# The quantised feed-forward of layer 2: one pipeline over four batch elements, with the depthwise convolution taken into three matmuls

## Chip, cores and metric

The kernel runs on one core of one Trainium2 chip. The metric is the device time of one execution in microseconds (us). It is a whole small model of some fourteen sublayers, and the change touches one of them, called L2f in the code.

## What is computed

Per batch element x is 512 tokens by 128 features, and there are four elements. L2f is a feed-forward with "bit-linear" layers (the reference, cut):

```python
def act_quant(x):                     # per token
    scale = 127.0 / clip(max(abs(x), axis=-1), 1e-05)
    return clip(round(x * scale), -128, 127) / scale
def weight_quant(w):                  # one scale for the matrix
    scale = 1.0 / clip(mean(abs(w)), 1e-05)
    return clip(round(w * scale), -1, 1) / scale
def bit_linear(x, w):
    return einsum('bsd,hd->bsh', act_quant(x), weight_quant(w))

h = bit_linear(x, w1)                 # 128 -> 512
h = depthwise_conv1d(h, conv_w, conv_b)   # 3 taps along the tokens, padding 1
h = silu(h)
return bit_linear(h, w2)              # 512 -> 128
```

The result is added to x and layer-normalised. All arithmetic of this part is float32.

## The kernel before, in words

Activations are kept feature-major: a tile has 128 features on the partitions and 512 tokens along the row. The program is a list of sublayers. Ahead of each, `turn` (L120) waits for that sublayer's weight pack, which lies in one of two arenas in SBUF, and issues the DMA of the next sublayer's pack into the other (L131). A sublayer is made of stages. A stage (`core.stage`, L116) is a block in which every engine runs its own list of instructions, ordered by semaphores; no engine goes on to the next stage before all have ended this one. Each engine is a queue in program order. `Chain` (L41) makes VectorE wait for each of its own instructions before the next, where the next reads what it wrote.

`each(bit_ffn)` (L3102) runs `bit_ffn` (L2972) for the four elements in turn, and then one residual-and-norm over all of them. For one element `bit_ffn` has six stages:

1. `quantize_weights` (L2884): ScalarE takes the absolute values of w1 and w2 with a running sum (L2900), TensorE adds the sums over the partitions (L2905), VectorE makes mean and inverse and quantises each 128x512 matrix in three passes: scale and round (L2915), subtract and clip (L2916), clip and scale back (L2917). It is done anew for each element, with the same result.
2. `quantize_tokens` (L2920) of x: TensorE transposes four 128x128 tiles so that tokens lie on the partitions (L2937); VectorE, tile after tile, takes the maximum (L2953), four operations on one column (L2955 to L2958) and three passes over the tile (L2959, L2961, L2962); when all four tiles are done TensorE transposes them back (L2943) and ScalarE copies them to SBUF (L2969).
3. `dense` (L224): four products with the chunks of w1, read out in turn by ScalarE and VectorE. A float32 product of 128x128 by 128x512 shows as two MATMUL records.
4. The convolution: VectorE, three passes for each of the four 128-feature chunks of the 512 hidden features (L2997, and L3000 twice); ScalarE applies SiLU to each chunk (L3012).
5. `quantize_tokens` of the hidden features: as stage 2 with sixteen transposes each way and tiles of 128x512.
6. `dense` with w2: four products added up in one bank, copied to `core.sums` (L261).

Of the kernel before, what the change touches and what calls it, by code (L numbers as in the profile page):

```python
# [8 lines left out]
P = 128  # L9
B, S, D = 4, 512, 128  # L10
TILE = 128
QT = S // TILE
# [2868 lines left out]
ROUND = 1.5 * 2.0 ** 23  # L2881


def quantize_weights(core, raw, out):  # L2884

    nc = core.nc
    with core.stage() as st, nc.sbuf_tensor(f"wq_abs{nc.next_id()}", [P, 2, 512], F32) as mag, \
            nc.sbuf_tensor(f"wq_sum{nc.next_id()}", [P, 2], F32) as sums, \
            nc.sbuf_tensor(f"wq_mean{nc.next_id()}", [P, 2], F32) as mean, \
            nc.sbuf_tensor(f"wq_inv{nc.next_id()}", [P, 2], F32) as inv:  # L2890
        sums_ready, total_ready, step = st.sem("sums_ready"), st.sem("total_ready"), st.sem("step")

        @st.block.sync
        def _(sp):
            sp.sem_clear(st.stale)

        @st.block.scalar
        def _(act):
            for i in range(2):
                nc.scalar.activation(mag[:, i, :], raw[i], ACT.Abs, accum_out=sums[:, i:i + 1]).then_inc(sums_ready, 1)  # L2900

        @st.block.tensor
        def _(pe):
            pe.wait_ge(sums_ready, 2)
            nc.tensor.matmul(core.ps[0][:, 0:2], core.c("ones"), sums[:, :], start=True, stop=True)\  # L2905
              .then_inc(total_ready, 1)

        @st.block.vector
        def _(dve):
            link = Chain(dve, step)  # L2910
            dve.wait_ge(total_ready, 1)
            link(nc.vector.tensor_scalar(mean[:, :], core.ps[0][:, 0:2], 1.0 / (P * 512), 1e-5, ALU.mult, ALU.max))
            link(nc.vector.reciprocal(inv[:, :], mean[:, :]))
            for i in range(2):
                link(nc.vector.tensor_scalar(out[i], raw[i], inv[:, i:i + 1], ROUND, ALU.mult, ALU.add))  # L2915
                link(nc.vector.tensor_scalar(out[i], out[i], ROUND, 1.0, ALU.subtract, ALU.min))  # L2916
                link(nc.vector.tensor_scalar(out[i], out[i], -1.0, mean[:, i:i + 1], ALU.max, ALU.mult))  # L2917


def quantize_tokens(core, src, dst, chunks):  # L2920

    nc = core.nc
    width = chunks * P
    with core.stage() as st, nc.sbuf_tensor(f"tq{nc.next_id()}", [P, QT, width], F32) as q, \
            nc.sbuf_tensor(f"tq_max{nc.next_id()}", [P, QT], F32) as top, \
            nc.sbuf_tensor(f"tq_scale{nc.next_id()}", [P, QT], F32) as scale:
        turned, step, quantized, back, evac = (st.sem(n) for n in ("turned", "step", "quantized", "back", "evac"))

        @st.block.sync
        def _(sp):  # L2930
            sp.sem_clear(st.stale)

        @st.block.tensor
        def _(pe):
            for t in range(QT):
                for c in range(chunks):
                    mm = nc.tensor.transpose(core.ps[t][:, c * P:(c + 1) * P], src[:, c, t * P:(t + 1) * P],  # L2937
                                             core.ident)
                mm.then_inc(turned, 1)
            pe.wait_ge(quantized, QT)  # L2940
            for c in range(chunks):
                for t in range(QT):
                    mm = nc.tensor.transpose(core.ps[4 + c][:, t * P:(t + 1) * P], q[:, t, c * P:(c + 1) * P],  # L2943
                                             core.ident)
                mm.then_inc(back, 1)

        @st.block.vector
        def _(dve):
            link = Chain(dve, step)
            for t in range(QT):  # L2950
                dve.wait_ge(turned, t + 1)
                one = slice(t, t + 1)
                link(nc.vector.tensor_reduce(top[:, one], core.ps[t][:, 0:width], AX_X, ALU.max,  # L2953
                                             apply_absolute_value=True))
                link(nc.vector.tensor_scalar(top[:, one], top[:, one], 1e-5, None, ALU.max))  # L2955
                link(nc.vector.reciprocal(scale[:, one], top[:, one]))
                link(nc.vector.tensor_scalar(scale[:, one], scale[:, one], 127.0, None, ALU.mult))
                link(nc.vector.tensor_scalar(top[:, one], top[:, one], 1.0 / 127.0, None, ALU.mult))  # L2958
                link(nc.vector.tensor_scalar(q[:, t, :], core.ps[t][:, 0:width], scale[:, one], ROUND,  # L2959
                                             ALU.mult, ALU.add))  # L2960
                link(nc.vector.tensor_scalar(q[:, t, :], q[:, t, :], ROUND, 127.0, ALU.subtract, ALU.min))  # L2961
                nc.vector.tensor_scalar(q[:, t, :], q[:, t, :], -128.0, top[:, one], ALU.max, ALU.mult)\  # L2962
                  .then_inc(quantized, 1)

        @st.block.scalar
        def _(act):
            for c in range(chunks):
                act.wait_ge(back, c + 1)
                nc.scalar.copy(dst[:, c, :], core.ps[4 + c][:, :]).then_inc(evac, 1)  # L2969


def bit_ffn(core, b, arena):  # L2972
    nc = core.nc
    w = core.weights("L2f", arena)
    M = 4
    with ExitStack() as mem:
        def tmp(name, shape):
            return mem.enter_context(nc.sbuf_tensor(f"l2f_{name}_{nc.next_id()}", shape, F32))
        W, xq = tmp("W", [P, 2, 512]), tmp("xq", [P, 1, S])
        h, z, hq = tmp("h", [P, M, S + 2]), tmp("z", [P, M, S]), tmp("hq", [P, M, S])  # L2980
        quantize_weights(core, [w("w1"), w("w2")], [W[:, i, :] for i in range(2)])
        quantize_tokens(core, core.X.unsqueeze(1), xq, 1)
        dense(core, M, lambda k, m: W[:, 0, m * P:(m + 1) * P], lambda k: xq[:, 0, :], lambda m: h[:, m, 1:S + 1])
        with core.stage() as st:
            step, conv_ready, silu_ready = (st.sem(n) for n in ("step", "conv_ready", "silu_ready"))

            @st.block.sync
            def _(sp):
                sp.sem_clear(st.stale)

            @st.block.vector
            def _(dve):
                link = Chain(dve, step)
                link(nc.vector.memset(h[:, :, 0:1], 0.0))
                link(nc.vector.memset(h[:, :, S + 1:S + 2], 0.0))
                for m in range(M):
                    link(nc.vector.tensor_scalar(z[:, m, :], h[:, m, 0:S], w("conv_w", 3 * m, 3 * m + 1),  # L2997
                                                 w("conv_b", m, m + 1), ALU.mult, ALU.add))
                    for j in (1, 2):
                        ins = nc.vector.scalar_tensor_tensor(  # L3000
                            out=z[:, m, :], in0=h[:, m, j:j + S], scalar=w("conv_w", 3 * m + j, 3 * m + j + 1),
                            in1=z[:, m, :], op0=ALU.mult, op1=ALU.add)
                        if j == 1:
                            link(ins)
                        else:
                            ins.then_inc(conv_ready, 1)

            @st.block.scalar
            def _(act):
                for m in range(M):  # L3010
                    act.wait_ge(conv_ready, m + 1)
                    nc.scalar.activation(z[:, m, :], z[:, m, :], ACT.Silu).then_inc(silu_ready, 1)  # L3012
# [185 lines left out]
def cols_of(v):  # L3198

    return v.reshape(-1, P).T  # L3200
# [51 lines left out]
def packs(x):  # L3252
# [158 lines left out]
```

## Time and profile before

| | |
|---|---|
| Runs shown | 5674.03, 5654.67, 5646.64 us; median 5654.67 |
| The profiled execution | 5665.67 us |
| Its span in the trace | 5663.4 us |
| TensorE busy, share of the span | 4616.4 us, 82% |
| VectorE | 3167.7 us, 56% |
| ScalarE | 2854.6 us, 50% |
| GpSimd | 1976.5 us, 35% |
| Mean granted TensorE clock | 0.883 of full speed |

The span is that of one execution as the hardware profiler saw it; 2.3 us of the time lie outside it. Busy times are of the whole program, so they say little about one sublayer; the views of the stretch from 4494 to 4726 us, in which L2f runs, do. In the traces PE is TensorE's matmuls, PEld its weight loads, DVE VectorE, ACT ScalarE, POOL GpSimd and SP the queue that issues the DMAs. A granted clock of 1.00 is 2.4 GHz and 0.50 is 1.2 GHz.

### The profile page before, as it was taken

To read this page: it belongs to the slowest core of one execution; us is meant where nothing else is said; L and a number is where in the kernel's file an instruction comes from. 1 tells how busy PE (TensorE), PEld (TensorE's weight loads), DVE (VectorE), ACT (ScalarE), POOL (GpSimd) and SP (SyncE) were. 2 spreads that over 40 slices of the span, in tenths; PEclk is the share of its full clock that TensorE was granted. 3 is DMA by queue.
4 is the path that set the end of the run, shared out by engine and by line. 5 is a ranking of instruction groups with operands and counts; after the bars stand their busy time and mean duration, and the time that the engine had idled before them with its cause. 6 is when DMAs were issued, how large, how long until landed. Compare 5 with 4: busy or idle time off the path is not lost. (4 is left out here: it accounts for less than half of the span.)

```text
span 5663.4 us, 100659 instructions
## 1 busy us (share of the span) xinstructions
PE 4616.4 (82%) x36210; PEld 2809.5 (50%) x36210; DVE 3167.7 (56%) x6182; ACT 2854.6 (50%) x8728; POOL 1976.5 (35%) x2119
## 2 busy tenths in 40 slices
PE   3998779997988979889798899655589736888888
PEld 1665346565655646646466465344466522224433
DVE  6452245455756747567476575399945554654333
ACT  2452234455756747667476574477724312543411
POOL 0230000136939839579396692033213200000000
PEclk6999979899999999999999998767689856997888
DMA  0000000001111111111112111000000000001000
GB/s 32 22 1 4 15 11 7 17 2 27 45 40 41 45 42 44 44 37 45 37 45 55 31 45 34 19 1 1 1 5 1 4 0 7 9 3 34 3 0 8
DMA packets 34488, 122.26 MB, mean 22 GB/s; under 512 B 8484, under 2 KB 9512, under 8 KB 32424
## 3 DMA queue, kind: packets, MB, share of 16 engines
q1 hardware_dynamic: 33960, 115.44, 7.6%
q8 instruction: 304, 4.98, 0.4%
q14 instruction: 224, 1.84, 0.1%
HBM read 36.45 MB, written 1.05 MB: 7 GB/s over the span
## 5 line engine op out<-in xcount | busy, mean ns | idle before, releaser
L640 POOL MEMSET norm_eps<- 128x1 f32 x16 | 1.6, 98 | 1920.0 <-POOLq L116 1861.0
L2095 POOL TENSOR_TENSOR local_other<-local_raw,local_sin 128x256 f32<-128x256 f32 x768 | 557.3, 726 | 60.2
L1956 PE MATMUL ps<-arena,local_xs 128*128 128x512 f32 x768 | 440.3, 658 | 109.5 <-DVE local_raw L2136 60.4
L2092 POOL TENSOR_TENSOR local_rot<-local_raw,local_cos 128x512 f32<-128x512 f32 x384 | 488.2, 1271 | 68.3 <-DVE local_raw L2136 68.2
L2098 POOL TENSOR_TENSOR local_rot<-local_rot,local_other 128x512 f32<-128x512 f32 x384 | 486.6, 1267 | 30.1
L2069 ACT ACTIVATE ps<-ps,local_negmax 128x96 f32<-128x96 f32 x1536 | 474.2, 309 | 41.0 <-DVE local_negmax L2130 41.0
L2136 DVE SCALAR_TENSOR_TENSOR local_raw<-local_inverse,ps 128x512 f32<-128x512 f32 x384 | 264.1, 688 | 274.1 <-ACT local_inverse L2063 274.1
L2126 DVE TENSOR_REDUCE local_norm<-local_squares 128x8 f32<-128x512 f32 x384 | 263.2, 685 | 133.6 <-ACT local_squares L2038 133.6
L2069 ACT ACTIVATION_READ_ACCUMULATOR ps<-ps,local_negmax 128x1 f32 x1536 | 309.8, 202 | 0.0
L2038 ACT ACTIVATE local_squares<-ps 128x512 f32<-128x512 f32 x384 | 229.8, 598 | 158.5 <-PE ps L1956 158.3
L2001 PE MATMUL ps<-const,local_probs 128*96 128x128 f32 x1536 | 237.0, 276 | 75.7 <-DVE local_probs L2154 75.7
L1985 PE MATMUL ps<-const,local_rot 128*128 128x128 f32 x1536 | 245.9, 282 | 45.1 <-POOL local_rot L2098 45.0
L1985 PEld LDWEIGHTS ps<-const,local_rot 128*128 128x128 f32 x1536 | 175.1, 141 | 188.0 <-POOL local_rot L2098 92.8
L2001 PEld LDWEIGHTS ps<-const,local_probs 128*96 128x96 f32 x1536 | 171.9, 126 | 192.6 <-DVE local_probs L2154 100.6
L2014 PE MATMUL ps<-local_pts,local_V_span 96*64 96x64 f32 x6144 | 266.5, 230 | 0.5
L2014 PEld LDWEIGHTS ps<-local_pts,local_V_span 96*64 96x64 f32 x6144 | 213.2, 139 | 71.0 <-issue 69.9
L2077 ACT COPY local_pts<-ps 96x512 f32<-96x512 f32 x384 | 221.4, 577 | 17.6 <-PE ps L2001 17.6
L1432 DVE TENSOR_REDUCE l3a_limits<-ps 128x1 f32<-128x512 f32 x256 | 165.0, 686 | 111.5 <-PE ps L1280 111.5
L2047 ACT ACTIVATE local_Q<-ps 128x512 f32<-128x512 f32 x192 | 114.6, 597 | 217.4 <-PE ps L1985 217.4
L2154 DVE TENSOR_TENSOR local_probs<-ps,local_total 128x384 f32<-128x384 f32 x384 | 214.1, 557 | 13.3
L2130 DVE TENSOR_REDUCE local_negmax<-ps 128x4 f32<-128x384 f32 x384 | 210.4, 548 | 7.4 <-PE ps L1974 7.4
L1956 PEld LDWEIGHTS ps<-arena,local_xs 128*128 128x128 f32 x768 | 119.4, 195 | 180.8 <-DVE local_raw L2136 105.1
(510 smaller groups left out, 11083.9 us busy)
## 6 DMA issues: line engine op xcount, KB each, us to landing
local_V_span<-local_V SPq DMA_DIRECT2D x96, 384.0 KB, 4.0
local_V_span<-local_V SPq DMA_DIRECT2D x96, 256.0 KB, 3.6
arena<-in_L1f_a SPq DMA_DIRECT2D x7, 2176.0 KB, 8.3
local_V_span<-local_V SPq DMA_DIRECT2D x72, 128.0 KB, 2.3
arena<-in_L3f SPq DMA_DIRECT2D x1, 3460.0 KB, 11.3
arena<-in_L1f_f SPq DMA_DIRECT2D x6, 537.5 KB, 3.9
arena<-in_L0f SPq DMA_DIRECT2D x1, 2824.5 KB, 9.9
arena<-in_L0x SPq DMA_DIRECT2D x1, 2049.5 KB, 9.1
```

The source lines that it names most:

```text
L1956: nc.tensor.matmul(bank("qk", n)[:, :], tokens_of(tile), w("Wqkv", QKV[i] * 512, (QKV[i] + 1) * 512), start=True, stop=True)\
L1985: mm = nc.tensor.transpose(TURN[:, c * P:(c + 1) * P], m.rot[:, n % 4, c * P:(c + 1) * P], core.ident)
L2001: mm = nc.tensor.transpose(PT[0:SPAN, u * P:(u + 1) * P], m.probs[:, g % 2, u, :], core.ident)
L2014: mm = nc.tensor.matmul(OUT[DH * h:DH * h + DH, c * SPAN_Q:(c + 1) * SPAN_Q], m.V_span[:, tile % 2, half_span, (2 * c + h) * DH:(2 * c + h ...
L2038: nc.scalar.activation(m.squares[:, n % 2, :], bank("qk", n)[:, :], ACT.Square).then_inc(squared, 1)
L2069: nc.scalar.activation(scores, scores, ACT.Exp, bias=m.negmax[:, s % 2, u:u + 1], accum_out=m.total[:, s % 2, u:u + 1])\
L2077: nc.scalar.copy(m.pts[:, g % 3, :, :].rearrange("p u q -> p (u q)"), PT[0:SPAN, :])\
L2092: link(nc.gpsimd.tensor_tensor(rot, raw, m.cos[:, t, a * DH:(a + 1) * DH].unsqueeze(1) .broadcast_to([P, 8, DH]), ALU.mult))
L2095: link(nc.gpsimd.tensor_tensor(other[:, :, lo:lo + HALF], raw[:, :, HALF - lo:DH - lo], m.sin[:, t, a * DH + lo:a * DH + lo + HALF].unsque ...
L2098: nc.gpsimd.tensor_tensor(rot, rot, other, ALU.add).then_inc(rotated, 1)
L2126: nc.vector.tensor_reduce(m.norm[:, n % 4, :], heads(m.squares[:, n % 2, :]), AX_X, ALU.add)\
L2136: nc.vector.scalar_tensor_tensor(out=heads(m.raw[:, n % 4, :]), in0=m.inverse[:, n % 4, :].unsqueeze(2).broadcast_to([P, 8, DH]), scalar=1 ...
```

## The change

- The list of sublayers names `bit_ffn_all` in the place of `each(bit_ffn)`. It has one stage for all four elements, followed by the same residual-and-norm.
- Weights are quantised once. The first matrix, quantised, is multiplied by the convolution's weights into three matrices `taps` (VectorE, three `tensor_tensor` of 128x512). For this the host puts `conv_rows`, 1536 columns, into the pack of L2f; the old `conv_w` stays in it.
- The first product and the convolution are one: for each chunk TensorE adds three products in one bank, one per tap, of `taps[j]` with the quantised x read from column j of a buffer of 514 columns whose edge columns are zero (GpSimd writes them). ScalarE applies SiLU with the bias as it reads the bank.
- The four single-column operations of a quantisation are done once for four tiles, on four columns.
- Every engine's order is written out for steps s = 0 to 4: TensorE does the products of element s, the transposes of its hidden features, then the transposes back and the second products of element s-1, and the transposes back of x for element s+1. VectorE quantises the hidden features of element s and then x of element s+2. Two banks of PSUM serve the first products and the transposes back in turn, four hold the transposed hidden features, one x and one the last product.

The core of the diff:

```diff
-def bit_ffn(core, b, arena):
-        quantize_weights(core, [w("w1"), w("w2")], [W[:, i, :] for i in range(2)])
-        quantize_tokens(core, core.X.unsqueeze(1), xq, 1)
-        dense(core, M, lambda k, m: W[:, 0, m * P:(m + 1) * P], lambda k: xq[:, 0, :], lambda m: h[:, m, 1:S + 1])
...
-        quantize_tokens(core, z, hq, M)
-        dense(core, 1, lambda k, m: W[:, 1, k * P:(k + 1) * P], lambda k: hq[:, k, :], lambda m: core.Y[:, :],
-              kcount=M)
+def bit_ffn_all(core, _, arena):
...
+            def convolve(b, m):
+                wait_bank(("hidden", b, m))
+                pe.wait_ge(x_read, b + 1)
+                for j in range(TAPS):
+                    mm = nc.tensor.matmul(place["hidden", b, m][:, :], taps[:, j, m * P:(m + 1) * P],
+                                          x_quant[:, b % 2, j:j + S], start=(j == 0), stop=(j == TAPS - 1))
+                mm.then_inc(hidden_ready, 1)
+
+            def turn_hidden(b):
+                pe.wait_ge(hidden_read, M * (b + 1))
+                for t in range(QT):
+                    if b >= 1:
+                        pe.wait_ge(tile_read, QT * (b - 1) + t + 1)
+                    for c in range(M):
+                        mm = nc.tensor.transpose(TURNED[t][:, c * P:(c + 1) * P], z[:, c, t * P:(t + 1) * P], core.ident)
+                    mm.then_inc(turned, 1)
+
+            def back_hidden(b, c):
+                wait_bank(("back", b, c))
+                pe.wait_ge(rows_ready, QT * (b + 1))
+                for t in range(QT):
+                    mm = nc.tensor.transpose(place["back", b, c][:, t * P:(t + 1) * P],
+                                             rows[:, b % 2, t, c * P:(c + 1) * P], core.ident)
+                mm.then_inc(back_ready, 1)
...
+            turn_x(0)
+            pe.wait_ge(sums_ready, 2)
+            nc.tensor.matmul(OUT[:, 0:2], core.c("ones"), sums[:, :], start=True, stop=True).then_inc(total_ready, 1)
+            back_x(0)
+            turn_x(1)
+            pe.wait_ge(edges, 2)
+            pe.wait_ge(taps_ready, TAPS)
+            for s in range(B + 1):
+                if s < B:
+                    for m in range(M):
+                        convolve(s, m)
+                        if m == 1 and s >= 1 and s + 1 < B:
+                            turn_x(s + 1)
+                    turn_hidden(s)
+                if s >= 1:
+                    if s == 1:
+                        pe.wait_ge(second_ready, 1)
+                    back_hidden(s - 1, 0)
+                    back_hidden(s - 1, 1)
+                    for c in range(M):
+                        if c + 2 < M:
+                            back_hidden(s - 1, c + 2)
+                        project(s - 1, c)
+                if s + 1 < B:
+                    back_x(s + 1)
...
+            def scales():
+                link(nc.vector.tensor_scalar(top[:, :], top[:, :], 1e-5, None, ALU.max))
+                link(nc.vector.reciprocal(scale[:, :], top[:, :]))
+                nc.vector.tensor_scalar(unit[:, :], top[:, :], 1.0 / 127.0, None, ALU.mult).then_inc(step, 1)
+                link.steps += 1
+                link(nc.vector.tensor_scalar(scale[:, :], scale[:, :], 127.0, None, ALU.mult))
...
+            def quantize_hidden(b):
+                for t in range(QT):
+                    dve.wait_ge(turned, QT * b + t + 1)
+                    link(nc.vector.tensor_reduce(top[:, t:t + 1], TURNED[t][:, :], AX_X, ALU.max,
+                                                 apply_absolute_value=True))
+                scales()
+                for t in range(QT):
+                    here, one = rows[:, b % 2, t, :], slice(t, t + 1)
+                    nc.vector.tensor_scalar(here, TURNED[t][:, :], scale[:, one], ROUND, ALU.mult, ALU.add)\
+                      .then_inc(tile_read, 1)
+                    dve.wait_ge(tile_read, QT * b + t + 1)
+                    link(nc.vector.tensor_scalar(here, here, ROUND, 127.0, ALU.subtract, ALU.min))
+                    nc.vector.tensor_scalar(here, here, -128.0, unit[:, one], ALU.max, ALU.mult).then_inc(rows_ready, 1)
+
+            quantize_x(0)
+            dve.wait_ge(total_ready, 1)
...
+            quantize_weights(0)
+            for j in range(TAPS):
+                nc.vector.tensor_tensor(taps[:, j, :], whole[:, 0, :], w("conv_rows", j * 512, (j + 1) * 512), ALU.mult)\
+                  .then_inc(taps_ready, 1)
+            quantize_x(1)
+            quantize_weights(1)
+            for b in range(B):
+                quantize_hidden(b)
+                if b + 2 < B:
+                    quantize_x(b + 2)
+    residual_norm_all(core, core.sums)
...
-             ("L2f", each(bit_ffn)), ("L3a", projected_attention), ("L3x", cross_narrow), ("L3f", each(experts))]
+             ("L2f", bit_ffn_all), ("L3a", projected_attention), ("L3x", cross_narrow), ("L3f", each(experts))]
...
+    p.add("conv_rows", np.tile(x["L2_ffn_conv_w"][:, 0, :].T.reshape(1, -1), (P, 1)))
```

ScalarE's list in the new stage: absolute sums of both matrices, the copy of x(0), then per step four SiLUs of element s, four copies of the transposed-back hidden features of element s-1, the copy of its result to `core.sums`, and the copy of x for element s+1.

## Rows read from the trace of the kernel before

**Rows 1.** Busy time by engine (count), granted clock, DMA share, GB/s, L2f's stretch.

```profile
4494.00:4726.00 232.00, 86.43 (x232) 51.36 (x232) 124.62 (x354) 35.96 (x66) 0.10 (x1) 0.59 0.01 2
```

**Rows 2.** Longest waits, 4494 to 4728 us: total, times, longest.

```profile
PE ps L2943 <- DVE tq L2962: 69.7, 8, 10.2
...
ACT l2f_hq L2969 <- PE ps L2943: 64.3, 16, 15.3
```

**Rows 3.** Timeline, element 0, and the last copy of element 3: start, duration.

```profile
4495.02 0.63 ACT L2900 ACTIVATE wq_abs<-arena 128x512 f32<-128x512 f32 x1 [2.74 <-PEq L122]
...
4509.29 1.12 PE L2943 MATMUL ps<-const,tq 128*128 128x128 f32 x4 [7.27 <-DVE tq L2962]
4510.45 0.58 ACT L2969 COPY l2f_xq<-ps 128x512 f32<-128x512 f32 x1 [14.10 <-PE ps L2943]
...
4511.34 5.46 PE L251 MATMUL ps<-l2f_xq,l2f_W 128*128 128x512 f32 x8 [0.93 <-PEq L116]
...
4527.31 3.65 PE L2937 MATMUL ps<-const,l2f_z 128*128 128x128 f32 x16 [10.50 <-PEq L116]
...
4529.92 0.75 DVE L2959 TENSOR_SCALAR tq<-ps,tq_scale 128x512 f32<-128x512 f32 x1
4530.71 0.43 DVE L2961 TENSOR_SCALAR tq<-tq 128x512 f32<-128x512 f32 x1
4531.17 0.49 DVE L2962 TENSOR_SCALAR tq<-tq,tq_max 128x512 f32<-128x512 f32 x1
4531.57 0.69 DVE L2953 TENSOR_REDUCE tq_max<-ps 128x1 f32<-128x512 f32 x1
...
4533.05 0.75 DVE L2959 TENSOR_SCALAR tq<-ps,tq_scale 128x512 f32<-128x512 f32 x1
...
4724.75 0.60 ACT L261 ACTIVATE sums<-ps 128x512 f32<-128x512 f32 x1 [6.11 <-PE ps L251]
```

**Rows 4.** Groups of VectorE by shape, 4494 to 4728 us: busy us, mean ns.

```profile
L3000 DVE SCALAR_TENSOR_TENSOR l2f_z<-l2f_h,arena,l2f_z 128x512 f32<-128x512 f32 x32 | 24.1, 752 | 1.1
...
L2959 DVE TENSOR_SCALAR tq<-ps,tq_scale 128x128 f32<-128x128 f32 x16 | 5.6, 351 | 0.6
...
L2962 DVE TENSOR_SCALAR tq<-tq,tq_max 128x128 f32<-128x128 f32 x16 | 4.6, 286 | 0.6
L2915 DVE TENSOR_SCALAR l2f_W<-arena,wq_inv 128x512 f32<-128x512 f32 x8 | 3.9, 487 | 0.3
L2961 DVE TENSOR_SCALAR tq<-tq 128x128 f32<-128x128 f32 x16 | 3.6, 227 | 0.6
```

**Rows 5.** Timeline, state-space sublayer L2a: products with shifted windows, SiLU with bias.

```profile
3578.81 7.03 PE L2463 MATMUL ps<-ssm_xn,ssm_taps 128*128 128x512 f32 x16
3585.68 1.88 PE L2466 MATMUL ps<-ssm_xn,arena 128*128 128x512 f32 x4
...
3577.29 0.69 ACT L2486 ACTIVATE ssm_XC<-ps,arena 128x512 f32<-128x512 f32 x1 [2.75 <-PE ps L2463]
```

**Rows 6.** Timeline, local attention: four transposes at full clock, and what follows.

```profile
2511.10 0.66 PE L1985 MATMUL ps<-const,local_rot 128*128 128x128 f32 x4
2511.59 0.59 PE L1992 MATMUL ps<-arena,local_xs 128*128 128x512 f32 x1
```

**Rows 7.** One line's instructions, L394 (elementwise product in SBUF): ns min/median/max.

```profile
L394 DVE TENSOR_TENSOR rwkv_num<-rwkv_num,rwkv_kv x4: 691/692/692, 28.7 to 113.7; 128x512 f32<-128x512 f32 x4
```

**Rows 8.** As Rows 1, microseconds after and long after products at L251.

```profile
4515.00:4516.00 1.00, 1.00 (x4) 0.49 (x3) 0.69 (x1) 0.02 (x1) 0.00 (x0) 1.00 0.00 0
4521.00:4522.00 1.00, 0.00 (x0) 0.00 (x0) 0.96 (x2) 0.00 (x0) 0.00 (x0) 0.89 0.00 0
```

**Rows 9.** Page, DMA issues (KB, us to landing), and the issue of L2f's pack.

```profile
arena<-in_L1f_a SPq DMA_DIRECT2D x7, 2176.0 KB, 8.3
...
arena<-in_L2f SPq DMA_DIRECT2D x1, 520.0 KB, 3.6
...
4172.23 0.33 SPq L131 DMA_DIRECT2D arena<-in_L2f  x1
```

More of the change, by code:

```diff
@@ L2881, with tmp @@
 ROUND = 1.5 * 2.0 ** 23
-def quantize_weights(core, raw, out):
+ROUND = 1.5 * 2.0 ** 23
+def bit_ffn_all(core, _, arena):
     nc = core.nc
[L2887 to L2891, printed above, removed]
+    w = core.weights("L2f", arena)
+    M, TAPS = 4, 3
+    TURNED, RING, ROWS, OUT = core.ps[0:4], core.ps[4:6], core.ps[6], core.ps[7]
+    uses = []
+    for s in range(B + 1):
+        uses += [("hidden", s, m) for m in range(M) if s < B] + [("back", s - 1, c) for c in range(M) if s >= 1]
+    place = {use: RING[n % 2] for n, use in enumerate(uses)}
+    held = {use: uses[n - 2] for n, use in enumerate(uses) if n >= 2}
+    with core.stage() as st, ExitStack() as mem:
+        def tmp(name, shape):
+            return mem.enter_context(nc.sbuf_tensor(f"l2f_{name}_{nc.next_id()}", shape, F32))
+        mag, sums, mean, inverse = tmp("mag", [P, 2, 512]), tmp("sum", [P, 2]), tmp("mean", [P, 2]), tmp("inverse", [P, 2])
+        whole, taps = tmp("whole", [P, 2, 512]), tmp("taps", [P, TAPS, 512])
+        x_rows, x_quant = tmp("x_rows", [P, 2, QT, P]), tmp("x_quant", [P, 2, S + 2])
+        z, rows, quant = tmp("z", [P, M, S]), tmp("rows", [P, 2, QT, 512]), tmp("quant", [P, M, S])
+        top, scale, unit = tmp("top", [P, QT]), tmp("scale", [P, QT]), tmp("unit", [P, QT])
+        step, sums_ready, total_ready, taps_ready, second_ready, edges, x_turned, x_ready, x_back, x_read = (
+            st.sem(n) for n in ("step", "sums_ready", "total_ready", "taps_ready", "second_ready", "edges", "x_turned",
+                                "x_ready", "x_back", "x_read"))
+        hidden_ready, hidden_read, turned, rows_ready, back_ready, back_read, projected, stored, tile_read = (
+            st.sem(n) for n in ("hidden_ready", "hidden_read", "turned", "rows_ready", "back_ready", "back_read",
+                                "projected", "stored", "tile_read"))
         @st.block.sync
@@ L2897, in _, with read_x @@
         @st.block.scalar
         def _(act):
[L2899 to L2906, printed above, removed]
+            def read_x(b):
+                act.wait_ge(x_back, b + 1)
+                nc.scalar.copy(x_quant[:, b % 2, 1:S + 1], ROWS[:, :]).then_inc(x_read, 1)
@@ new lines, in _ @@
+            for i, name in enumerate(("w1", "w2")):
+                nc.scalar.activation(mag[:, i, :], w(name), ACT.Abs, accum_out=sums[:, i:i + 1]).then_inc(sums_ready, 1)
+            read_x(0)
+            for s in range(B + 1):
+                if s < B:
+                    for m in range(M):
+                        act.wait_ge(hidden_ready, M * s + m + 1)
+                        if m == 0 and s >= 1:
+                            act.wait_ge(turned, QT * s)
+                        nc.scalar.activation(z[:, m, :], place["hidden", s, m][:, :], ACT.Silu,
+                                             bias=w("conv_b", m, m + 1)).then_inc(hidden_read, 1)
+                if s >= 1:
+                    for c in range(M):
+                        act.wait_ge(back_ready, M * (s - 1) + c + 1)
+                        if c == 0 and s >= 2:
+                            act.wait_ge(projected, s - 1)
+                        nc.scalar.copy(quant[:, c, :], place["back", s - 1, c][:, :]).then_inc(back_read, 1)
+                    act.wait_ge(projected, s)
+                    nc.scalar.copy(core.sums[:, s - 1, :], OUT[:, :]).then_inc(stored, 1)
+                if s + 1 < B:
+                    read_x(s + 1)
@@ L2910, in _ @@
             link = Chain(dve, step)
-            dve.wait_ge(total_ready, 1)
[L2912 to L2917, printed above, removed]
@@ L2920, in quantize_tokens @@
[L2920 to L2969, printed above, removed]
@@ new lines, in quantize_weights @@
+            def quantize_weights(i):
+                out = whole[:, i, :]
+                link(nc.vector.tensor_scalar(out, w(("w1", "w2")[i]), inverse[:, i:i + 1], ROUND, ALU.mult, ALU.add))
+                link(nc.vector.tensor_scalar(out, out, ROUND, 1.0, ALU.subtract, ALU.min))
+                ins = nc.vector.tensor_scalar(out, out, -1.0, mean[:, i:i + 1], ALU.max, ALU.mult)
+                if i == 0:
+                    link(ins)
+                else:
+                    ins.then_inc(second_ready, 1)
@@ new lines, in _ @@
+            quantize_x(0)
+            dve.wait_ge(total_ready, 1)
+            link(nc.vector.tensor_scalar(mean[:, :], OUT[:, 0:2], 1.0 / (P * 512), 1e-5, ALU.mult, ALU.max))
+            link(nc.vector.reciprocal(inverse[:, :], mean[:, :]))
+            quantize_weights(0)
[3 more added lines that the diff above has]
+            quantize_x(1)
```

79 lines of the change are left out of this document (45 added, 34 removed).

## The prediction

> **What bounds the kernel now.** I read the busy times of the sublayer's stretch first, then its waits, then the timeline of one element. In the 232 us of L2f no engine comes near its limit: VectorE is busy 124.6 us (54%), TensorE 86.4 (37%), ScalarE 36.0, with TensorE's clock at a mean of 0.59 [rows 1]. So the work is a chain handed from engine to engine. The waits say the same: TensorE stood 69.7 us in eight waits for VectorE's quantising, and ScalarE 64.3 us for transposes whose own release was that quantising [rows 2]. The reader is to see waits that all end on the engine before in the chain, and none on a DMA. The chain runs from ScalarE's first instruction at 4495.02 to the end of the last copy at 4724.75 + 0.60 = 4725.35, thus 230.3 us, four times some 57.6 [rows 3]. What counts is how long the new chain is between these two points; the program before and after is the same.
>
> **Prices.** A float32 product of 128x512 at full clock: sixteen records (eight products) from 3578.81 to 3585.68, 0.86 us each [rows 5]; those are products with windows shifted by single columns, as here. At half clock twice that, 1.71. A transpose at full clock: four from 2511.10 to 2511.59, 0.12 each, 0.49 for four [rows 6]; at half clock sixteen take 3.65 with their end, about 0.21 each [rows 3]. From the end of four slow transposes (0.85) to ScalarE's read: 4510.45 - 4509.29 - 0.85 = 0.31 us, taken for each read of a bank [rows 3]. A copy 0.58, SiLU with bias out of PSUM 0.69 [rows 3, 5]; I add 0.05 to each for the signal back. VectorE on 128x512: from start to start 0.79 for the first pass (it reads PSUM), 0.46 the second, 0.40 the third where the next does not need it; maximum plus four column operations 4533.05 - 4531.57 = 1.48, of which 0.72 the maximum and 0.19 each of the four [rows 3]. On 128x128: 0.35, 0.23 and 0.29 [rows 4], 0.99 for the three with 0.04 for each link.
>
> **The change part by part**, times from the first instruction (0), at full clock unless said.
>
> Start. x(0) is turned (1.2, clock low); maximum and column operations 1.5 (the four columns of 128 are one reduction of 512 elements); twelve passes 4 x 0.99 = 4.0; mean and inverse 0.4. TensorE's sum over the absolute values lies under this. w1 in three passes of 0.53 + 0.46 + 0.53 = 1.5, by 487 ns for the outer ones [rows 4] and 0.46 for the middle. **The three products into `taps`** are new: nearest row 692 ns, 2.1 for three [rows 7]. If they cost as the slowest two-input pass here, 0.75, it is 0.2 more; below 0.69 no row of that size goes, and even at nothing it is 2.1 less. The sum is 10.7. The transposes back and the copy of x(0), 2.1, end under w1. ScalarE's table load can cost 1.3 at most, and ScalarE has idle time there.
>
> Products of element 0: 12 x 0.86 = 10.3. Before, eight records starting at 4511.34 went from low clock to high, and the microsecond from 4515 had it at 1.00 [rows 3, 8]; so about 3.5 us go at half speed, 1.75 more, to 22.8. The last SiLU 0.31 + 0.69 + 0.05 = 1.05, and `turn_hidden(0)` starts at 23.8. Sixteen transposes 1.96, x(1) back and copied 0.49 + 0.31 + 0.63 = 1.4, products of element 1 with x(2) turned among them 10.3 + 0.5, SiLU 1.05: `turn_hidden(1)` starts at 39.0. x(1) and w2, 6.9 us on VectorE, are done by 17.6 and so cost nothing; their cover is the products of element 0.
>
> One step from there: transposes 1.96; two chunks back 0.98; the third needs the bank of the first, 0.31 + 0.63 after it, so 0.46 of waiting; the rest 2 x 0.49 + 4 x 0.86 = 4.4; then the products of the next element wait for x, and ScalarE's copy of it stands behind the copy of the result: 0.31 + 0.65 + 0.63 = 1.6; products and x turned 10.8; SiLU 1.05. Together **21.3 us on TensorE**. VectorE in one step: four maxima 2.9, columns 0.76, four tiles of 1.65 = 6.6, together 10.3; x 5.5; sum 15.8. It fits, and each wait is met: quantised rows are needed some 21 us after the turn begins and are ready after 11, and x(s+2) is turned in the middle of the products and ready 5.5 later, before the next hidden tile comes. The new wait of `turn_hidden` for `tile_read` has behind it on TensorE the whole of the next step, but VectorE has read those tiles 10 us before. So turns start at 39.0, 60.3 and, without an x to turn, 81.1.
>
> End. After the last turn VectorE needs 0.8 + 10.3, until 92.1, and TensorE, done with element 2 at 88.9, stands 3.2. Then 5.9 for chunks and products and 0.9 for the copy: **98.9 us**, in the place of 230.3. Saved: 131.4.
>
> Off the path: the convolution's 12 passes per element on VectorE (L2997, and L3000 of 752 ns [rows 4]) and 24 stages less 1 with their boundaries are in the 230.3 and need no term. SP: the pack of L2f grows by 1536 columns, 768 KB, to 1288 KB. 520 KB landed 3.6 us and 2176 KB 8.3 us after issue, and L2f's is issued at 4172.23, over 300 us before its use [rows 9]: nothing. The next pack is issued as before at the head of the sublayer, and 99 us cover it. GpSimd's two small memsets are under the first 10 us.
>
> The profiled execution took 5665.67 us, of which its span is 5663.4; less 131 it is 5534. The median of the runs shown is 11.0 below it, 5654.67; less 131 it is **5524 us**.
>
> **The rivals.**
> (A) The clock doesn't stay. Between the products of one element and the next there are 1.05 of waiting, 1.96 and 0.98 of transposes and 0.46 of waiting, 4.4 us without a product, and before the last chunks 3.2 us of idleness. For it: in the old kernel sixteen transposes from 4527.31 ran their whole 3.65 us at half clock, and the clock fell within 4521 to 4522 after some 5 us without work [rows 3, 8]. Against it: here TensorE works in 17.6 of 21.3 us, and its waits are 1.6 at most until the end. Priced with everything but the products of w1 at half clock: turns 4 x 1.5, chunks back and second products (10.3 for 5.9) 4 x 4.5, and each of three later elements climbs anew, 3 x 1.75: 29 us, so 5553. The rule of the Trainium skill, "TensorE: Matmul & The Clock Gate", section "A second HAM failure mode: psum-queue depth-cycling", speaks for this rival: short idle times between groups of matmuls that rotate through PSUM banks can make the clock go back and forth. By that rule the time would be nearer 5553 than 5524; no row here shows such a rotation with full 128-row products losing the clock. If the clock stayed low all the time: products of w1 4 x 20.6, turns 13.6, chunks and second products 41, and 22 of waits: 159 us, 5583.
> (B) The elements don't overlap, because a wait in one of the three hand-written orders stands ahead of what the other engine needs (VectorE has the hidden features of b ahead of x of b+2). Then each element costs its own chain, 8 + 13 + 11 + 7 = 39, and 156 in all: 5580. I find no such wait.
> (C) Slower than before: TensorE reading x_quant from an odd column is slow. Place: the 48 products of `convolve`, 96 records of 0.43 us. To end 0.5% slower the stage would have to take 258 us, 159 more than reckoned, 1.7 per record: it decides from 2.1 us for a record, five times the price. At ten times it would be 371 us more than my sum, about 5895. Against it stands the L2a stage, which reads windows at one-column steps at 0.86 a product [rows 5].
> (D) It saves what it says only in part: if the quantised weights alone counted, some 6 us for each of three elements, 18 of 5655, that is no change.
>
> **How the numbers follow.** Forecast 0.76; (A) 0.14; clock low throughout or (B) 0.05; (D) or something of its size 0.03; (C) 0.02. Range: below, the sum may be wrong by 2.1 for taps and by the 0.31 and 0.05 counted in some 25 reads, 8 us together, and the median of a few runs lies some 8 us about its place (the runs shown spread over 27): 5508. Above it takes in (A) and some of that spread: 5565. Changes of 0.5%, 28 us, are about what a measurement of this kernel can tell: faster than 5626 in all but (C) and (D).
>
> **What would show it.** The stretch of L2f is 99 us (95 to 130) from the first absolute sum to the last copy to `sums`, in one stage; SiLUs of successive elements 21 us apart; TensorE over 80% busy at a clock near 1.00 from some 4 us after the first product; the largest waits of VectorE for `turned`, of TensorE for the first element's taps (10 us) and for the last rows (3 us). Wrong if the records of the products are far from 0.43 us apart, if the clock in the steps is under 0.9 (A), if the SiLU groups come over 30 us apart (B), or if other sublayers change by more than a few us.

## The result, and the profile after

The changed kernel took 5528.99 us, median of four runs (5521.40 to 5533.31), against 5659.44 for the kernel before in four (5646.64 to 5674.03). The ratio is 0.9767, 95% interval 0.974 to 0.9795. Forecast was 5524 us and, against the median then known, a ratio of 0.977.

The profiled execution has 5529.55 us and a span of 5527.8, 135.6 less than before. Where those 135.6 us lie is read from the stretch of L2f, from ScalarE's first absolute sum to the end of the last copy to `sums`. ScalarE's timeline of the changed kernel (start, duration, in brackets the idle time before and its releaser) has its ends:

```profile
4499.73 0.63 ACT L3015 ACTIVATE l2f_mag<-arena 128x512 f32<-128x512 f32 x1 [2.74 <-PEq L122]
...
4545.48 0.59 ACT L3032 COPY sums<-ps 128x512 f32<-128x512 f32 x1 [1.99 <-PE ps L2977]
...
4566.11 0.58 ACT L3032 COPY sums<-ps 128x512 f32<-128x512 f32 x1 [1.99 <-PE ps L2977]
...
4586.31 0.58 ACT L3032 COPY sums<-ps 128x512 f32<-128x512 f32 x1 [1.99 <-PE ps L2977]
...
4597.86 0.58 ACT L3032 COPY sums<-ps 128x512 f32<-128x512 f32 x1 [2.04 <-PE ps L2977]
```

4598.44 - 4499.73 = 98.7 us, where it was 230.3 [rows 3]: 131.6 less, of 131.4 foretold. The first three results come 20.6 and 20.2 us apart, the last after 11.6. The other 4.0 us are outside and not the change's: up to L2f the execution was 4.7 slower, the attention of layer 3 4.0 slower, its cross-attention 15.0 faster, the rest 2.3 slower. More of that below.

The busy times of the same stretch in the changed kernel (columns as in [rows 1]: us, then busy time and count for PE, PEld, DVE, ACT, POOL, then clock, DMA share, GB/s), whole, in the steps, and at the end:

```profile
4499.73:4598.44 98.71, 82.08 (x290) 44.54 (x290) 62.42 (x159) 27.17 (x45) 0.11 (x2) 0.90 0.01 4
...
4514.00:4579.00 65.00, 59.00 (x210) 30.58 (x209) 40.67 (x101) 18.22 (x29) 0.00 (x0) 1.00 0.00 0
4579.00:4587.00 8.00, 7.04 (x39) 4.49 (x37) 7.26 (x15) 2.83 (x5) 0.00 (x0) 1.00 0.00 1
4587.00:4598.00 11.00, 8.06 (x24) 4.95 (x24) 2.49 (x5) 2.48 (x5) 0.00 (x0) 0.69 0.01 1
```

TensorE has about as much busy time as before (82.1 us, where it was 86.4) in 43% of the time: it now does three times the first products, but mostly at full clock (mean 0.90, where it was 0.59 [rows 1]). VectorE's busy time is halved. In the 65 us of the steps TensorE is busy 91%, and the clock 1.00 throughout.

From the waits of the stretch (total, times, longest): those of TensorE, which sets the step, are small.

```profile
ACT l2f_z L3023 <- PE ps L2952: 37.7, 16, 5.2
...
DVE l2f_top L3075 <- PE ps L2962: 18.5, 3, 9.9
...
PE ps L2945 <- DVE l2f_x_rows L3056: 4.5, 1, 4.5
PE ps L2969 <- DVE l2f_rows L3084: 3.5, 1, 3.5
PE ps L2962 <- ACT l2f_z L3023: 3.1, 4, 0.8
...
PE ps L2952 <- ACT l2f_x_quant L3012: 2.4, 3, 0.8
```

ScalarE and VectorE now wait for TensorE. Before, TensorE waited 69.7 us for VectorE's quantising [rows 2], and 57.8 us more, ahead of its transposes, for the other engines to end the stage before (PEq L116 is TensorE's queue at the head of a stage), here by the waits of the kernel before:

```profile
PE ps L2937 <- PEq L116: 57.8, 8, 10.5
```

TensorE's own timeline of the changed kernel, one step and the end:

```profile
4537.83 1.97 PE L2962 MATMUL ps<-const,l2f_z 128*128 128x128 f32 x16 [0.78 <-ACT l2f_z L3023]
4539.63 1.04 PE L2969 MATMUL ps<-const,l2f_rows 128*128 128x128 f32 x8
4540.91 0.66 PE L2969 MATMUL ps<-const,l2f_rows 128*128 128x128 f32 x4 [0.24 <-ACT l2f_quant L3030]
4541.40 1.02 PE L2977 MATMUL ps<-l2f_quant,l2f_whole 128*128 128x512 f32 x2
4542.26 0.60 PE L2969 MATMUL ps<-const,l2f_rows 128*128 128x128 f32 x4
4542.70 2.74 PE L2977 MATMUL ps<-l2f_quant,l2f_whole 128*128 128x512 f32 x6
4545.28 0.60 PE L2945 MATMUL ps<-const,l2f_x_rows 128*128 128x128 f32 x4
4546.70 5.39 PE L2952 MATMUL ps<-l2f_x_quant,l2f_taps 128*128 128x512 f32 x12 [0.82 <-ACT l2f_x_quant L3012]
4551.92 0.60 PE L2938 MATMUL ps<-const,tokens 128*128 128x128 f32 x4
4552.36 5.32 PE L2952 MATMUL ps<-l2f_x_quant,l2f_taps 128*128 128x512 f32 x12
4558.45 1.98 PE L2962 MATMUL ps<-const,l2f_z 128*128 128x128 f32 x16 [0.78 <-ACT l2f_z L3023]
...
4589.76 2.88 PE L2969 MATMUL ps<-const,l2f_rows 128*128 128x128 f32 x12 [3.48 <-DVE l2f_rows L3084]
4592.43 1.92 PE L2977 MATMUL ps<-l2f_quant,l2f_whole 128*128 128x512 f32 x2
```

From one `turn_hidden` (L2962) to the next 20.6 us pass, of which 1.84 are waits: 0.24 for a bank, 0.82 for x, 0.78 for the last SiLU. At 4589.76 begins the end: twelve transposes take 2.67 us until the next group starts, 0.22 each, the price at half clock; the granted clock of these 2.67 us is 0.50.

### The profile page after: what moved, and what is told of

Its sections match the earlier page's. It is cut to its first block and busy times, and to the rows that moved or that the text cites. A ratio compares the mean times of both kernels' runs of the same rounds, so it can differ in the third digit from the quotient of the medians.

```text
span 5527.8 us, 100339 instructions
## 1 busy us (share of the span) xinstructions
PE 4611.5 (83%) x36268; PEld 2805.7 (51%) x36268; DVE 3103.6 (56%) x5989; ACT 2846.3 (51%) x8708; POOL 1976.2 (36%) x2121
## 5 line engine op out<-in xcount | busy, mean ns | idle before, releaser
L2014 PEld LDWEIGHTS ps<-local_pts,local_V_span 96*64 96x64 f32 x6144 | 213.6, 139 | 70.9 <-issue 69.7
```

The costliest lines, as they stand in the source:

```text
L2014: mm = nc.tensor.matmul(OUT[DH * h:DH * h + DH, c * SPAN_Q:(c + 1) * SPAN_Q], m.V_span[:, tile % 2, half_span, (2 * c + h) * DH:(2 * c + h ...
```

## The experiments

Two theories stood against each other in the runs. Mine: the gain is the overlap of engines and elements, so that the parts of the change, taken alone, are small. The rival: one part (weights once, or the tap products) carries it. What is compared is the stretch as read above, since it is short and came out the same to 0.1 us in the second execution of two kernels, while the time of the whole wanders by 30 us and more. The wholes stand beside it, medians where there are several runs; the kernel before had medians of 5649 to 5659 us in the same measurements.

| Kernel | Stretch, us | Whole, us (runs) |
|---|---|---|
| before | 230.3 | 5659.4 (4) |
| e1, e12: weights once | 209.4, 209.3 | 5643.5 (10), 5632.0 (1) |
| e3: scales of four tiles | 206.4 | 5630.5 (1) |
| e2: weights once, tap products | 199.1 | 5622.9 (1) |
| e10: all three, stage by stage | 177.9 | 5603.7 (1) |
| e5: one stage, one element's hidden features at a time | 136.7 | 5565.7 (4) |
| e4: pipeline, convolution on VectorE | 118.3 | 5558.3 (1) |
| e6: pipeline, scales tile by tile | 102.5 | 5543.4 (1) |
| after; e11: once more | 98.7, 98.8 | 5529.0 (4), 5519.2 (1) |
| e7: clock kept at the end | 96.2 | 5518.7 (1) |
| e8: orders changed | 90.7 | 5521.7 (4) |
| e9: two tap products left out | 76.0 | 5521.8 (1) |

**e1_weights_once.**

```diff
+        quantize_weights(core, [w("w1"), w("w2")], [W[:, i, :] for i in range(2)])
+        for b in range(B):
+            core.work_on(b)
+            bit_ffn(core, b, arena, W)
...
-        quantize_weights(core, [w("w1"), w("w2")], [W[:, i, :] for i in range(2)])
```

> The kernel before with one change: the weights are quantised once instead of four times. My theory (the saving comes from the overlap of elements, and the repeated weights are a small part): the weights' stage takes 5.9 us from the first absolute sum to the first transpose, so three of them go, the stretch from the first absolute sum to the last copy to sums falls from 230.3 to 212.7 us, and the whole by 0.3%. Rival (the repeated weights are the main thing): over 60 us less.

The stretch is 209.4, 21.0 less: the rival falls. I had reckoned 17.6. Of the other 3.4 us, 2.2 lie in element 0, whose work is as before: its second products took 3.67 us, the price at full clock, where they took 5.34. The mean clock in the stretch is 0.62 against 0.59. The whole, however, had a ratio of 0.9995 (0.9974 to 1.0016), and this interval leaves out the 0.996 that was due. Three of the ten runs took 5675 to 5681 us and seven 5628 to 5647, beside thirteen runs of the kernel before from 5645 to 5660. In the profiled execution, one of the three, the cross-attention of layer 3 took 263.6 us against 238.1; e12 takes this up.

**e2_taps_by_stages**, on e1:

```diff
-        dense(core, M, lambda k, m: W[:, 0, m * P:(m + 1) * P], lambda k: xq[:, 0, :], lambda m: h[:, m, 1:S + 1])
+        dense(core, M, lambda k, m: taps[:, k, m * P:(m + 1) * P], lambda k: xq[:, 0, k:k + S], lambda m: z[:, m, :],
+              kcount=3, func=ACT.Silu, bias=lambda m: w("conv_b", m, m + 1))
```

and the VectorE convolution removed.

> As e1, and the convolution made of three products per chunk with the tap matrices, still stage after stage and element after element. Theory: per element two stages of together 16 us (first products, convolution) become one of about 13.8, and the transposes after it find the clock high, 1.5 less; the new tap stage costs 3 once. The stretch is about 204 us, 9 less than e1: moving the convolution to TensorE is worth little while nothing overlaps. Rival (the tap products carry the gain by themselves): 8 us per element, under 185 us.

199.1: 10.2 less than e1, near my 9 and far from the rival's 8 per element. Twelve VectorE passes per element went, and eight products on TensorE took nearly their whole time, one behind the other.

**e3_scales_alone**, on the kernel before: the maxima of all four tiles first, then L2955 to L2958 once on four columns.

> The kernel before with one change: the four column operations of a quantisation are done for four tiles at once. Theory: 12 operations of 0.19 us less in each of eight quantisations, all on the chain: 18 us less, less about 0.3 us for waiting for the fourth tile each time, the stretch 213 to 215 us against 230.3. Rival (the columns are hidden behind the transposes): 230.

206.4: 24.0 less, 7 to 9 more than the 213 to 215 that were expected. In TensorE's groups of this kernel the second products have a mean of 601 ns (full clock) where before they had 867; first the groups of e3, then that of the kernel before:

```profile
L251 PE MATMUL ps<-l2f_xq,l2f_W 128*128 128x512 f32 x32 | 24.1, 923 | 3.7 <-PEq L116 3.7
...
L251 PE MATMUL ps<-l2f_hq,l2f_W 128*128 128x512 f32 x32 | 14.7, 601 | 3.7 <-PEq L116 3.7
```

```profile
L251 PE MATMUL ps<-l2f_hq,l2f_W 128*128 128x512 f32 x32 | 22.5, 867 | 3.7 <-PEq L116 3.7
```

So 7.8 us of TensorE's busy time went by the clock, which now had risen when the second products came, and the column operations themselves are worth some 16. That the shorter stage ahead moved the moment of the rise fits, but is not shown: in e1 the second products of element 0 took 3.67 us and those of element 1 5.77, behind the same pause of 10.14 us and the same 3.68 us of transposes.

**e10_all_by_stages**: e2 with the edit of e3.

> e2 (weights once, convolution as tap products, stage after stage) with the scales of four tiles at a time as in e3. Theory: the three savings lie one behind the other on the same chain and add up: 199.1 less 24.0 = 175 us. What then separates it from e5 (136.7, one stage, elements not overlapped) is stage boundaries and the overlap inside one element, 38, and from e5 to the changed kernel the overlap of elements, 38. Rival (they overlap in effect, for instance through the clock): off by more than 5 us.

177.9, 2.8 off the sum of the parts: 21.3 for the scales here. The parts are additive to that 2.8, as they should be in a chain, and with all three 52.5 of the 131.6 us are had. The other 79.1 come with the single stage and its orders.

**e5_no_overlap**: the changed kernel, in which TensorE and ScalarE take `back_hidden` and `project` of element s, not s-1, after `turn_hidden(s)`.

```diff
-            for s in range(B + 1):
+            for s in range(B):
...
-                    back_hidden(s - 1, 0)
-                    back_hidden(s - 1, 1)
+                back_hidden(s, 0)
+                back_hidden(s, 1)
```

> The changed kernel, but TensorE and ScalarE finish an element (transposes back and second products too) before they begin the next. Theory: each element then waits 10.4 us for VectorE's quantising, with the clock falling: about 12 + 3 x 14 for the products, 4 x 20 for the rest and 10 for the start, 144 us; 130 if the clock stays high. So overlap is worth 30 to 45 us of the 131.6. Rival (one stage in the place of 24 and the tap products do it all): within 5 us of 98.7.

136.7: 41.2 below e10 and 38.0 above the changed kernel. TensorE stands 9.12 us in each element for the quantised rows, as this kernel's timeline shows:

```profile
4551.17 1.97 PE L2962 MATMUL ps<-const,l2f_z 128*128 128x128 f32 x16 [0.78 <-ACT l2f_z L3020]
4562.27 2.88 PE L2969 MATMUL ps<-const,l2f_rows 128*128 128x128 f32 x12 [9.12 <-DVE l2f_rows L3080]
4564.94 1.10 PE L2977 MATMUL ps<-l2f_quant,l2f_whole 128*128 128x512 f32 x2
```

My 144 was too high by the clock: it fell in each pause, but rose again within the twelve slow transposes and the first products, so that the next element's first products ran at full speed (0.43 a record). Mean clock in the elements 0.83. The whole: ratio 0.9875 (0.9813 to 0.9937).

The kernel's name says more than it does: x of the next element is still quantised under the work of the one before. From the end of an element's second products to the first products of the next, 9.0 us pass in e10 (first fence) and 1.3 in e5 (second fence), 7.7 less, three times:

```profile
4534.98 6.09 PE L251 MATMUL ps<-l2f_hq,l2f_W 128*128 128x512 f32 x8 [0.93 <-PEq L116]
...
4550.04 12.26 PE L251 MATMUL ps<-l2f_xq,l2f_taps 128*128 128x512 f32 x24 [0.93 <-PEq L116]
```

```profile
4535.42 2.74 PE L2977 MATMUL ps<-l2f_quant,l2f_whole 128*128 128x512 f32 x6
...
4539.42 5.39 PE L2952 MATMUL ps<-l2f_x_quant,l2f_taps 128*128 128x512 f32 x12 [0.82 <-ACT l2f_x_quant L3010]
```

So about 23 of the 41 us between e10 and e5 lie where x is quantised, and most of them are overlap of elements too; a kernel with one stage and no overlap at all was not run.

So the 131.6 us are, in this order of taking them: weights once 21, tap products 10, scales 21, one stage in which x is quantised ahead 41, hidden features of successive elements overlapped 38. No single part carries it.

**e4_vector_conv**: the changed kernel with one product per chunk, ScalarE's copy to `h`, three VectorE passes per chunk ahead of `quantize_hidden(b)`, and SiLU after them.

> The changed kernel with the convolution back on VectorE: one product per chunk, ScalarE copies it to SBUF, VectorE makes the three passes, ScalarE applies SiLU; the pipeline is otherwise kept. Theory: VectorE becomes the bound with 8.2 us of passes more per element, a step of some 25 us, the stretch 115 to 122 us against 98.7. TensorE works only 11 us in a step, so its clock may fall. Rival (tap products are worth nothing in the pipeline, since VectorE had room): 100 us or less.

118.3, as expected: in the pipeline the tap products are worth 19.5 us, twice what they are worth stage by stage (10.2), because there VectorE's list, and not TensorE's, sets most of the step: the first three steps take 25.9, 26.8 and 21.2 us against 14.9, 20.6 and 20.2 in the changed kernel. Part of it is the clock, since VectorE waits 9.2 us in all for transposes that mostly run at half clock. Between 4515 and 4595 VectorE is busy 82% and TensorE 49%, its clock 0.72:

```profile
4515.00:4595.00 80.00, 39.20 (x164) 26.76 (x164) 65.92 (x136) 22.60 (x40) 0.00 (x0) 0.72 0.00 0
```

**e6_scales_by_tile**: in the changed kernel the maximum and the four column operations are done per tile, directly ahead of its three passes.

> The changed kernel with the column operations done tile by tile again. Theory: VectorE needs 20.4 us in a step instead of 15.8, still under TensorE's 20.6, so only the start and the end grow, 2.3 us each: 103 us against 98.7. Rival (VectorE becomes the bound): each of three steps some 2 us longer as well, 108 or more.

102.5: the steps stay at 20.6 and 20.2 (copies to `sums` at 4551.30, 4571.93, 4592.13), and it is the start (2.7 us to the first copy to `sums`) and the end (1.1) that grow. The four-column scales, 21 us on the chain, are worth 3.8 where TensorE covers them.

**e7_keep_clock.**

```diff
+                    if s == B:
+                        for _ in range(4):
+                            nc.tensor.matmul(ROWS[:, :], taps[:, 0, 0:P], x_quant[:, (B - 1) % 2, 0:S], start=True, stop=True)
                     back_hidden(s - 1, 0)
```

> The changed kernel with four products into an unused bank ahead of the last element's transposes back, in the 3.5 us for which TensorE stands there (they add nothing to the result). Theory: the slow last part (8.1 us for sixteen transposes and four products, where it was 5.6 in the steps before) is the clock, which fell in those 3.5 us; with it kept high the stretch is 96.2 to 96.6 us against 98.7. Rival (the last part is slow for another reason, the copies for instance): 98.7 or more.

96.2, 2.5 less with work added. Of this, 0.3 lie ahead of the edit: the first 24 records took 11.93 us here and 12.19 in the changed kernel. The part behind the pause took 5.8 us instead of 8.1, so the idle products are worth 2.2. The timeline of this kernel shows the same transposes and products at full clock behind the four idle ones:

```profile
4580.66 3.60 PE L3001 MATMUL ps<-l2f_x_quant,l2f_taps 128*128 128x512 f32 x8
4584.30 1.07 PE L2969 MATMUL ps<-const,l2f_rows 128*128 128x128 f32 x8
4585.60 0.66 PE L2969 MATMUL ps<-const,l2f_rows 128*128 128x128 f32 x4 [0.24 <-ACT l2f_quant L3033]
```

Twelve transposes and a bank wait take 1.8 us here against 2.67.

**e8_reordered**: `turn_hidden` of elements 1 and 2 after the second products of the element before, `back_x(s + 1)` ahead of the last second product and its copy ahead of that to `sums`, the taps of the first chunk made first, and e7's products.

```diff
+                        if c == M - 1 and s + 1 < B:
+                            back_x(s + 1)
                         project(s - 1, c)
+                    if s < B - 1:
+                        turn_hidden(s)
```

> The changed kernel with its orders changed so that TensorE's short waits are filled: x is transposed back before the last second product, and the turn of the hidden features of elements 1 and 2 comes after the second products of the element before; the first chunk's taps are made first; four idle products keep the clock at the end as in e7. Theory (TensorE is the bound of a step): steps of 18.4 instead of 20.6 us twice, 1.3 less in the first step, 1.9 at the start, 2.3 at the end: 89 us against 98.7, 0.2% of the whole, which the time can hardly show and the trace can. Rival (VectorE's chain of quantising sets the step): 94 or more.

90.7, where 89 was expected, and 18.7 us from the turn of element 1 (4536.57) to that of element 2 (4555.28), where 18.4 was: the bound of a step is TensorE, whose waits in it are now 0.34. Of the 1.9 us at the start 1.0 came. Eight us in 5529 are 0.15%: the four runs, 5504.3 to 5567.7 with a median of 5521.7, have a ratio of 0.9775 (0.9718 to 0.9832) to the kernel before, so the time can't tell it from the changed kernel. It is the best stretch that computes the whole, not a shown improvement of the time.

**e9_one_tap**: one tap product per chunk in the place of three, so this kernel leaves out two thirds of the convolution.

> The changed kernel with two of the three tap products left out (the middle tap alone is computed), so TensorE has 6.9 us less work per element. Theory (TensorE bounds a step, VectorE has 4.8 us of room in it): the step falls only to what VectorE needs, some 16 to 17 us, and the stretch to about 77 us. If the clock needs TensorE this busy (11 of 16 us here against 17.6 of 20.6), it shows under 1.00 in the steps, and the stretch is 80 to 85. Rival (TensorE is not the bound): 95 or more.

76.0, and the turns (4532.61, 4547.61, 4562.68) are 15.0 apart. Here TensorE waits for VectorE within the turn and for the rows, and the clock stayed:

```profile
4533.00:4565.00 32.00, 25.57 (x119) 14.57 (x117) 29.88 (x77) 12.13 (x20) 0.00 (x0) 1.00 0.00 1
```

VectorE is busy 93%: it is the next bound, 5.6 us below TensorE's.

**e11_after_again and e12_once_again**, unedited repeats.

> The changed kernel once more, unedited, to see how far the time outside the stretch wanders. Theory (the clock in the cross-attention of layer 3, with its products of 32 rows, is a matter of each execution, not of the kernel): the stretch is 98.7 again within 0.5 us, and that sublayer takes anything between 219 and 264 us, in steps that go with its granted clock. Rival (the kernel sets it): 223 again, as in the first execution.

> e1 once more, unedited. Its stretch was 21 us shorter but its time the same as before, since the cross-attention of layer 3 took 263.6 us in its profile against 238.1. Theory (chance of the execution): stretch 209.4 again and the sublayer elsewhere in the range of 219 to 264. Rival (weights once moves everything after it to a bad place for the clock every time): 255 or more again.

The stretches are 98.8 and 209.3. The cross-attention of layer 3, from the issue of the next pack's DMA to the first gate of the experts, took 226.0 and 225.9 us (5519.20 and 5632.00 for the whole). For e1's kernel that is 38 us less than in its first execution, so the 263.6 were that execution's. The span of e12, 5629.1, is 34.3 below that of before: 21.1 in the stretch, 12.2 in that sublayer, 1.0 elsewhere. So in the profiled execution of e1 the cross-attention hid the 21 us. For the other two runs of 5675 us and more there is no trace, and that weights once brings 0.4% to the whole over many runs is not shown.

## Why the prediction was right, step by step

**The chain as the bound of before, and its price of 230.3.** Right: with the work reshaped and nothing overlapped, the parts add up to 2.8 us (e1, e2, e3, e10).

**The sum**, from the first instruction, foretold and measured:

| Step | Foretold | Measured |
|---|---|---|
| Taps ready, products of element 0 begin | 10.7 | 10.2 |
| `turn_hidden` of 0, 1, 2, 3 begins | 23.8, 39.0, 60.3, 81.1 | 23.2, 38.1, 58.7, 78.9 |
| One step on TensorE | 21.3 | 20.6 |
| The last rows are ready | 92.1 | 90.0 |
| The end of the last copy | 98.9 | 98.7 |

The total is closer than its terms. The forecast was 0.5 us too late at the taps and 0.9 at the turn of element 1, and each of its two steps behind that was 0.6 to 0.7 too long: 0.16 in the sixteen transposes (1.80, not 1.96), 0.16 in the first two chunks with the wait for a bank (1.28, not 1.44), 0.18 in the wait for x (1.42, not 1.6), 0.13 behind the last SiLU. That made 2.1 by the time of the last rows. The end was foretold as 6.8, at full clock, and took 8.7; this was named as part of rival (A), and e7 puts 2.2 on the clock. Two errors of opposite sign cancelled, and that is luck.

**Three products into `taps`.** From row 692 ns I took 2.1; they took 1.9, since they don't wait for each other and overlap by 0.08 each.

**VectorE fits into the step.** Right: 15.4 of 20.6 us; e6, which adds 4.6, leaves the steps as they were, and e9 shows the bound behind it.

**Shifted windows (C).** Six products from 4546.70 to 4551.92 are 0.87 each, as in L2a [rows 5]. The rival is refuted.

**The elements don't overlap (B).** Refuted by the 20.6 us steps. e5 built that case: 136.7, not the 156 that I had reckoned, since I had charged each element for the quantising of x, which stays hidden under other work there.

**The clock (A).** In the steps it was 1.00 from 4514 to 4579, with 4.3 us from the last first product of an element to the first second product of the one before, filled in part by transposes. The section "A second HAM failure mode: psum-queue depth-cycling" of the Trainium skill's page "TensorE: Matmul & The Clock Gate" tells of a bf16 kernel whose short idle times under such rotation through banks make the clock go back and forth. In this float32 pipeline, with waits of 0.24 to 0.82 us, the trace doesn't show it, with TensorE busy 91% in the steps, nor with 80% in e9. The clock of 0.72 in e4 says nothing on that rule, since TensorE stands there for 6.9 to 16.5 us at a time. Rival (A) came true at the very end alone: in the pause of 3.5 us before the last rows the clock fell some 2 us after TensorE's last record, which ends at 4586.28:

```profile
4588.00:4589.00 1.00, 0.00 (x0) 0.00 (x0) 0.97 (x2) 0.00 (x0) 0.00 (x0) 0.67 0.00 0
```

The prediction had that pause (3.2 us) in its sum at full clock, by a row in which the clock had fallen after some 5 us; that term was too small.

**The waits named as signs.** VectorE's for `turned` came. TensorE's for the first element's taps, foretold as 10 us, did not: its waits up to there were 4.5 us for the rows of x(0) and 0.8 for the taps, with transposes of x between them.

**The packs' DMA.** The pack of 1288 KB landed 7.2 us after issue, over 300 us ahead of its use: nothing, as said.

**Outside.** I had it unchanged; it was 5433.1 before and 5429.1 after in the two profiled executions. By the prediction's own last sign, other sublayers changing by more than a few us, it would have been wrong, since the cross-attention of layer 3 was 15.0 faster. But that moves without any edit: the changed kernel once more (e11) had 5418.6 outside, and over the kernels here it lies between 5418.6 and 5463.3. A sign of a few us was too narrow for a program that wanders so.

## What to carry over

A part's worth depends on the chain that it stands in: the four-column scales were worth 21 us on the chain and 3.8 under TensorE's cover, the tap products 10 on the chain and 20 in the pipeline, where they relieve its bound. Before building a pipeline, sum each engine's work for one element with the waits of its hand-written order; the largest sum was the step, to 0.7 us. And at the very end, where an engine stands idle for a last result, work that is of no use can pay by keeping the clock up.

## What the runs showed that I had not expected

The cross-attention of layer 3, which no kernel here edits, takes between 219 and 264 us for the same instructions, and the longer the lower its granted clock. Its busy times (columns as above) in the changed kernel, in e1 and in e7:

```profile
4986.44:5209.50 223.06, 188.42 (x1309) 91.85 (x1310) 90.93 (x213) 90.29 (x174) 4.75 (x5) 0.82 0.08 23
```

```profile
5092.49:5356.10 263.61, 230.74 (x1309) 108.51 (x1310) 93.31 (x213) 90.28 (x174) 4.76 (x5) 0.67 0.06 20
```

```profile
4980.93:5199.70 218.77, 183.96 (x1309) 91.43 (x1310) 91.15 (x213) 90.50 (x174) 4.76 (x5) 0.84 0.08 23
```

In e1 it spends 150 us near the low level while TensorE counts as busy 91% of the time, and 100% from 5226 to 5266:

```profile
5206.00:5356.00 150.00, 136.90 (x591) 62.67 (x584) 42.23 (x103) 44.94 (x89) 0.10 (x1) 0.53 0.01 3
```

In L2f, with products of 128 rows, the clock rose within 4 us of the first product; here 768 of the 1309 records have 32 rows, and it can stay down for long. Whether the rows decide it was not tried. It has the widest range over the fourteen profiled executions, 45 us (23 without that of e1), a third of what this change brought; the program before L2f has one of 20. A change of 20 us, as e1, drowns in that: it has to be read in its own stretch.
